# x loaded by column block and turned by VectorE, with single shares and half low pieces, in a fused GRU and mixture FFN kernel

## The chip, the cores and the metric

The kernel runs on one core of a Trainium2 chip. The metric is device time in microseconds of one execution; the median of three runs of the kernel before is 142.57 us (142.33 to 142.85). The engines that the text speaks of are TensorE (PE, with PEld for its weight loads), VectorE (DVE), ScalarE (ACT), GpSimd (POOL) and SyncE (SP), which here only issues DMAs.

## The reference

The input x has 32 sequences of 32 steps and 256 features. A GRU runs over the steps, and a feed-forward layer with routing is applied to the hidden states; x is added to its result.

```python
def cell(h, x):
    gi = x @ W_ih + b_ih
    gh = h @ W_hh + b_hh
    ...
    r = jax.nn.sigmoid(i_r + h_r)
    z = jax.nn.sigmoid(i_z + h_z)
    n = jnp.tanh(i_n + r * h_n)
    h_new = (1.0 - z) * n + z * h
...
probs = jax.nn.softmax(xt @ w_router, axis=-1)
topk_p, topk_idx = jax.lax.top_k(probs, TOPK)
...
gate = (xt @ w_gate).reshape(T, K, I)
up = (xt @ w_up).reshape(T, K, I)
basis = jax.nn.silu(gate) * up
...
out = out + shared
...
x = x + _L0_ffn_ref(_L0_cond_ref(cond_2048, x, ...), ...)
```

Here the batch is 32, the hidden size 256, there are 128 experts over 8 basis blocks of 128, and the best 4 are taken.

## The kernel before

The GRU is a chain of 32 steps. The state lies with 32 rows for each of four column blocks of 64 (j = 0 to 3), so that all 128 partitions are used. In a step t, `h_part` on TensorE (L618) adds h @ W_hh to a PSUM bank `gates` that already holds the part of x and the biases; ScalarE takes the tanh of two gates (`trz`, L415); VectorE makes `m` (L867), `pre` (L870) and the blend (`sc_add`, L873); ScalarE takes a second tanh (L422); VectorE runs a scan that blends (L879), transposes the new state into `hT` (L886) and halves it (`hhalf`, L887). Then the next `h_part` can start.

The feed-forward layer works on chunks of four steps, 128 rows. It trails the GRU by six steps: what `filler` puts on TensorE begins in step 6 with the `logits` (L651) and the first `unit` (L639). Each unit multiplies with a high and a low piece of the weights: ScalarE rounds a piece of `wraw` into `whi` (`hi_pieces`, L433), and VectorE (`lo_piece`, L899) or GpSimd (L341) subtracts it into `wlo`. The tables HI_AT, LO_VECTOR_AT and LO_POOL_AT say in which step which piece is made.

Steps 0 to 5 have no feed-forward work, and TensorE uses them to multiply x with W_ih ahead for the 18 steps in EARLY (`early_x_pair`, L597, two steps to a PSUM bank). VectorE adds the biases to each pair and keeps it in `early` (`keep_early`, L854); ScalarE loads it back into a `gates` bank in time. For the other steps `x_part` (L582) does this in the step before.

x comes in by chunks of four steps as `xtok` (L247), one row of 1 KB to a partition, eight loads of 128 KB. For the products it has to be turned: TensorE transposes a chunk with an identity (`turn_x`, L557), chunks 2 to 7 in pairs in steps 1 to 3, and VectorE (L832, L838) or, for one pair, ScalarE (L409) copies it into `xT`. `xtok` is also what the residual adds at the end (L996).

The order on each engine is written out by hand: in step t every engine does its part of the step, then `prepare(t)`, then the part of the feed-forward layer that trails. DMAs go over two hardware queues, SyncE's and ScalarE's, in program order: SyncE loads the first chunk of x, half of W_ih, W_hh in two parts, the second chunk, then waits for its half of W_ih, loads the other chunks, the router and the weights; ScalarE loads the other half of W_ih, the two biases and the first state `h0`. Before step 0, TensorE runs matmuls on zeros (`keep_warm`, L772), the x parts of steps 0 and 1 and the spreading of the biases over the banks (L550).

## Time and profile before

| | us |
|---|---|
| median of three runs | 142.57 (142.33 to 142.85) |
| the profiled execution | 142.47 |
| its span in the trace | 140.7 |
| start of step 0's h_part | 9.34 |
| start of step 6's h_part | 29.42 |

The span is what the trace covers, from the first instruction to the last; 1.8 us of the execution lie around it. The stages are read best one behind the other: loading up to 9.34 us, six steps of the GRU with the shares of x up to 29.42, then GRU and feed-forward layer together up to about 121, and the last chunk. In a table by stage each engine has its busy time and its count of instructions; PEclk is the clock that was granted, as a share of the full 2.4 GHz, and the DMA share is the mean over the core's 16 DMA engines. In a timeline a row has its start, its duration and, in brackets, how long the engine had been idle and what ended that. Durations of instructions that follow each other overlap a little, so what one costs its engine is the distance to the next start, called a slot here.

### The profile page before, as it was taken

Reading aid. Unit: us, or ns where it says so; the run is one execution under the profiler, and the core shown is the slowest. Engines: PE = TensorE matmul, PEld = TensorE weight load, DVE = VectorE, ACT = ScalarE, POOL = GpSimd, SP = SyncE. Lnnn points to the kernel's source line nnn. Section 1 sums busy time; section 2 is a strip of 40 time slices with the busy share of each in tenths; the row PEclk is TensorE's granted clock in tenths of the full one; section 3 lists DMA queues with packets and bytes.
Section 4 is the critical chain, followed back from the end, with each engine's and each line's share of the span. In section 5 each row is a group of like instructions: output and inputs, shape, how many; then the busy total and the mean of one; then the engine's idle time right before and its main releaser. Section 6 shows DMA issues by size and latency. Waiting matters only on the chain.

```text
span 140.7 us, 4037 instructions
## 1 busy us (share of the span) xinstructions
PE 135.4 (96%) x1485; PEld 98.3 (70%) x1485; DVE 105.4 (75%) x387; ACT 73.3 (52%) x246; POOL 70.0 (50%) x127
## 2 busy tenths in 40 slices
PE   6998999999999999999999999999999999999981
PEld 5455677666677667777777777777767776888880
DVE  1227699998779989885888588858885888686661
ACT  1214764667855565565556545655555554442930
POOL 5031165666656676534554454455545544885130
PEclk9999999999999999999999999999999999999997
DMA  4999980000000000000100010001000000010102
GB/s 127 315 298 306 310 301 13 0 5 2 0 5 0 0 2 5 2 0 5 37 0 0 5 37 0 9 0 37 0 5 0 31 11 0 2 37 0 42 0 75
DMA packets 5575, 7.12 MB, mean 51 GB/s; under 512 B 676, under 2 KB 4020, under 8 KB 5556
## 3 DMA queue, kind: packets, MB, share of 16 engines
q1 hardware_dynamic: 5184, 6.42, 13.8%
q10 hardware_dynamic: 308, 0.43, 1.2%
q8 instruction: 12, 0.20, 0.6%
q14 instruction: 7, 0.06, 0.1%
q0 software_dynamic: 64, 0.01, 0.0%
HBM read 5.81 MB, written 1.05 MB: 49 GB/s over the span
## 4 chain that ended last, share of the span: by engine, by line
PE 84%; DVE 10%; ACT 2%; issue 1%; DVEq 0%
PE unit L639 41%; PE gates L618 17%; PE gates L582 6%; PE down L701 5%; PE turned L772 3%; PE route L651 2%; DVE sc_out L879 2%; DVE early L854 2%; DVE wlo L899 2%; ACT sc_add L422 1%; PE route L674 1%; PE unit L597 1%; DVE hT L886 1%; DVE pre L870 1%; PE route L656 1%
## 5 line engine op out<-in xcount | busy, mean ns | idle before, releaser
L304 POOL CAST hThi<-hT 128x64 fp32r<-128x64 f32 x32 | 10.1, 316 | 50.5 <-DVE hT L886 50.5
L639 PE MATMUL unit<-whi,hThi 128*128 128x512 f32 x80 | 34.4, 430 | 0.0
L639 PE MATMUL unit<-wlo,hThi 128*128 128x512 f32 x80 | 31.6, 395 | 0.0
L639 PE MATMUL unit<-whi,hTlo 128*128 128x512 f32 x80 | 31.6, 395 | 0.0
L618 PE MATMUL gates<-whh,hT 128*32 128x192 f32 x512 | 27.4, 332 | 0.8 <-DVE hT L886 0.5
L415 ACT ACTIVATE trz<-gates 128x128 f32<-128x128 f32 x32 | 8.8, 276 | 24.6 <-PE gates L618 24.6
L618 PEld LDWEIGHTS gates<-whh,hT 128*32 128x32 f32 x512 | 13.4, 109 | 9.7 <-DVE hT L886 3.9
L639 PEld LDWEIGHTS unit<-whi,hThi 128*128 128x128 f32 x80 | 15.3, 192 | 6.6 <-issue 3.7
L879 DVE TENSOR_TENSOR_SCAN sc_out<-sc_mul,sc_add 128x128 f32<-128x128 f32 x32 | 14.0, 437 | 6.8 <-ACT sc_add L422 6.3
L639 PEld LDWEIGHTS unit<-wlo,hThi 128*128 128x128 f32 x80 | 15.0, 188 | 3.6
L928 DVE SCALAR_TENSOR_TENSOR p<-th,unit 128x256 f32<-128x256 f32 x40 | 15.9, 410 | 1.5 <-ACT th L443 1.5
L639 PEld LDWEIGHTS unit<-whi,hTlo 128*128 128x128 f32 x80 | 15.1, 189 | 2.1
L422 ACT ACTIVATE sc_add<-pre 128x64 f32<-128x64 f32 x32 | 10.3, 323 | 10.2 <-DVE pre L870 10.2
L316 POOL TENSOR_TENSOR qc<-q,coef 128x512 f32<-128x512 f32 x14 | 14.6, 1041 | 0.5 <-DVE q L940 0.5
L443 ACT ACTIVATE th<-unit 128x256 f32<-128x256 f32 x40 | 14.2, 370 | 1.0 <-PE unit L639 1.0
L867 DVE SCALAR_TENSOR_TENSOR m<-trz,gates 128x64 f32<-128x64 f32 x32 | 7.0, 217 | 8.5 <-ACT trz L415 8.2
L306 POOL TENSOR_TENSOR hTlo<-hT,hThi 128x64 fp32r<-128x64 f32 x32 | 11.6, 362 | 2.6
L582 PE MATMUL gates<-wih,xT 128*32 128x192 f32 x224 | 11.7, 327 | 0.0
L940 DVE SCALAR_TENSOR_TENSOR q<-p,unit 128x256 f32<-128x256 f32 x28 | 11.1, 415 | 0.5
L341 POOL TENSOR_TENSOR wlo<-wraw,whi 128x256 fp32r<-128x256 f32 x14 | 11.1, 816 | 0.0
L873 DVE SCALAR_TENSOR_TENSOR sc_add<-trz,hhalf 128x64 f32<-128x64 f32 x32 | 11.0, 343 | 0.0
L417 ACT ACTIVATE sc_mul<-trz 128x64 f32<-128x64 f32 x32 | 10.2, 320 | 1.0
(131 smaller groups left out, 238.5 us busy)
## 6 DMA issues: line engine op xcount, KB each, us to landing
xtok<-in_x_dram SPq DMA_DIRECT2D x8, 128.0 KB, 3.4
wraw<-in_L_ffn_w_gate_dram SPq DMA_DIRECT2D x2, 512.0 KB, 5.5
wraw<-in_L_ffn_w_up_dram SPq DMA_DIRECT2D x2, 512.0 KB, 6.5
out_dram<-ot SPq DMA_DIRECT2D x8, 128.0 KB, 2.0
whh<-in_L_cond_W_hh_dram SPq DMA_DIRECT2D x1, 512.0 KB, 6.2
wih<-in_L_cond_W_ih_dram ACTq DMA_DIRECT2D x1, 384.0 KB, 3.3
wih<-in_L_cond_W_ih_dram SPq DMA_DIRECT2D x1, 384.0 KB, 4.0
whh<-in_L_cond_W_hh_dram SPq DMA_DIRECT2D x1, 256.0 KB, 5.2
```

The source lines that it names most:

```text
L306: pool.tensor_tensor(hTlo[:, c % 3, :, :, k], hT[:, c % 2, :, k, :], hThi[:, c % 3, :, :, k].bitcast(F32), ALU.subtract).then_inc(hTlo_rea ...
L316: pool.tensor_tensor(qc[:, cols].rearrange("p (k i) -> p k i", i=I), q[:, p % 2, cols].rearrange("p (k i) -> p k i", i=I), coef[:, p % 2, ...
L341: last = pool.tensor_tensor(wlo[:, s, a, cols], wraw[:, s, a, cols], whi[:, s, a, cols].bitcast(F32), ALU.subtract)
L422: act.activation(by_block(sc_add, 0), natural(pre, slice(0, FJ)), ACT.Tanh).then_inc(n_ready, 1)
L443: act.activation(th[:, n % 2, :], unit_bank[n % NB][:, 0:UW], ACT.Tanh, scale=0.5)\
L582: pe.matmul(g[Q * j:Q * (j + 1), R:4 * FJ], x_block(t, s), wih[:, s, :].rearrange("p (g j c) -> p j g c", g=3, j=NJ)[:, j], start=False, s ...
L618: last = pe.matmul(g[Q * j:Q * (j + 1), HN:HN + 3 * FJ], st, whh[:, s, :].rearrange("p (g j c) -> p j g c", g=3, j=NJ)[:, j], start=False, ...
L639: last = pe.matmul(dst, st[:, p % 3, s, :, :].rearrange("p b t -> p (b t)"), w[:, s, :, cols], start=(s == 0 and n == 0), stop=(s == KB - ...
L873: dve.scalar_tensor_tensor(out=by_block(sc_add, 1), in0=natural(trz, slice(FJ, 2 * FJ)), scalar=1.0, in1=natural(hhalf, slice(0, FJ)), op0 ...
L879: dve.tensor_tensor_scan(sc_out[:, :, :].rearrange("p f a -> p (f a)"), sc_mul[:, :, :].rearrange("p f a -> p (f a)"), sc_add[:, :, :].rea ...
L928: dve.scalar_tensor_tensor(out=p1[:, n % 2, :], in0=th[:, n % 2, :], scalar=1.0, in1=unit_bank[n % NB][:, 0:UW], op0=ALU.add, op1=ALU.mult)\
L940: dve.scalar_tensor_tensor(out=dst, in0=p1[:, n % 2, :], scalar=0.5, in1=unit_bank[n % NB][:, UW:2 * UW], op0=ALU.mult, op1=ALU.mult).then ...
```

## The change

A second copy of x, `xj`, is loaded by column block: the 32 sequences of block j lie on partitions 32j to 32j + 31, with 64 floats for each step. It comes in five parts by steps (X_PARTS: 0 to 3, 4 to 7, 8 to 15, 16 to 23, 24 to 31), each by four DMAs, one to a block, in runs of 256 bytes. In this layout a transpose of 32 by 32 blocks on VectorE (`turn_x(n)`) gives `xT` directly. TensorE's transposes of x, `keep_x` and `keep_x_pair` on VectorE and ScalarE, and their semaphores are gone. `xtok` stays for the residual and is loaded last.

The first part of xj goes over both queues, two blocks each, ahead of everything else; part 1 follows W_hh on SyncE, parts 2 and 3 stand between W_ih's wait and the router, part 4 between the first and the second pair of weights.

The 18 early steps are now single shares, three in each of steps 0 to 5 (EARLY_SHARES), and the banks are handed out by a table (EARLY_BANK); VectorE keeps pairs 0 to 6 in steps 0 to 5 and pairs 7 and 8 in steps 11 and 12 (KEEP_EARLY). VectorE's three low pieces are made in halves (gate or up), over steps 3 to 6. Ahead of step 0, six warming matmuls stand where three and the first two transposes were, and the wait for the constants is behind the first products.

```diff
-EARLY_PAIRS = [[0], [1], [2], [3, 4], [5, 6], [7, 8]]
-TURN_PAIR = {1: 2, 2: 4, 3: 6}
-KEEP_PAIR_SCALAR = {1: 2}
-KEEP_PAIR_VECTOR = {2: 4, 3: 6}
+EARLY_SHARES = [[0, 1, 2], [3, 4, 5], [6, 7, 8], [9, 10, 11], [12, 13, 14], [15, 16, 17]]
+EARLY_BANK = [0, 1, 2, 0, 1, 2, 0, 3, 4]
+KEEP_EARLY = {0: [0], 1: [1], 2: [2, 3], 3: [4], 4: [5], 5: [6], 11: [7], 12: [8]}
+X_PARTS = [(0, 4), (4, 8), (8, 16), (16, 24), (24, 32)]
+TURN_X = {0: 2, 1: 3, 3: 4}
 HI_AT = [(0, 0), (0, 0), (0, 2), (2, 4), (4, 6), (6, 8), (8, 10)]
-LO_VECTOR_AT = [[], [], [], [2], [4], [5]]
+LO_VECTOR_AT = [[], [], [], [(2, 0)], [(2, 1), (4, 0)], [(4, 1), (5, 0)], [(5, 1)]]
...
+        def load_xj(queue, n, blocks=range(NJ)):
+            t0, t1 = X_PARTS[n]
+            for j in blocks:
+                queue.dma_start(xj[Q * j:Q * (j + 1), t0:t1, :], x[:, t0:t1, FJ * j:FJ * (j + 1)]).then_inc(ld_xj[n], 16)
...
-            return xT[:, t // TC, s, B * (t % TC):B * (t % TC + 1)]
+            return xT[:, s, B * t:B * (t + 1)]
...
-            load_x(sp, 0, 1)
+            load_xj(sp, 0, [0, 1])
             sp.dma_start(wih[:, 1, :], pairs(w_ih)[:, 1, :]).then_inc(ld_wih[1], 16)
             sp.dma_start(whh[:, :, 0:D], pairs(w_hh)[:, :, 2 * D:3 * D]).then_inc(ld_whh, 16)
             sp.dma_start(whh[:, :, D:3 * D], pairs(w_hh)[:, :, 0:2 * D]).then_inc(ld_whh, 16)
-            load_x(sp, 1, 2)
+            load_xj(sp, 1)
             sp.wait_ge(ld_wih[1], 16)
-            load_x(sp, 2, NC)
+            load_xj(sp, 2)
+            load_xj(sp, 3)
...
+                if pair == 0:
+                    load_xj(sp, 4)
...
+            load_x(sp, 0, NC)
...
+            load_xj(act, 0, [2, 3])
             act.dma_start(wih[:, 0, :], pairs(w_ih)[:, 0, :]).then_inc(ld_wih[0], 16)
...
-                if t in KEEP_PAIR_SCALAR:
-                    keep_x_pair(KEEP_PAIR_SCALAR[t])
...
+                pe.wait_ge(x_turned, 1 + [a <= t < b for a, b in X_PARTS].index(True))
...
+            def early_share(i):
+
+                n, a, t = i // 2, i % 2, EARLY[i]
+                dst = early_bank[EARLY_BANK[n]]
+                if i == 0:
                     pe.wait_ge(bias_ready, 1)
-                if n >= len(early_bank):
-                    pe.wait_ge(early_ready, n - len(early_bank) + 1)
-                for a, t in enumerate(EARLY[2 * n:2 * n + 2]):
-                    wait_x(t)
-                    for s in range(KB):
-                        for j in range(NJ):
-                            last = pe.matmul(dst[Q * j:Q * (j + 1), 4 * FJ * a + R:4 * FJ * (a + 1)], x_block(t, s),
-                                             wih[:, s, :].rearrange("p (g j c) -> p j g c", g=3, j=NJ)[:, j],
-                                             start=(s == 0), stop=(s == KB - 1), skip_group_check=True)
-                last.then_inc(early_raised, 1)
-
-            def turn_x_pair(c):
-                wait_x(TC * (c - 1))
-                turn_x(c, route, 0)
-                turn_x(c + 1, route, 1)
+                if a == 0 and EARLY_BANK[n] in EARLY_BANK[:n]:
+                    pe.wait_ge(early_ready, 1 + max(m for m in range(n) if EARLY_BANK[m] == EARLY_BANK[n]))
+                wait_x(t)
+                for s in range(KB):
+                    for j in range(NJ):
+                        last = pe.matmul(dst[Q * j:Q * (j + 1), 4 * FJ * a + R:4 * FJ * (a + 1)], x_block(t, s),
+                                         wih[:, s, :].rearrange("p (g j c) -> p j g c", g=3, j=NJ)[:, j],
+                                         start=(s == 0), stop=(s == KB - 1), skip_group_check=True)
+                if a == 1:
+                    last.then_inc(early_raised, 1)
...
-                if t < len(EARLY_PAIRS):
-                    for n in EARLY_PAIRS[t]:
-                        early_x_pair(n)
-                if t == 0:
-                    turn_x(1, unit_bank[2], 0)
-                if t in TURN_PAIR:
-                    turn_x_pair(TURN_PAIR[t])
+                if t < len(EARLY_SHARES):
+                    for i in EARLY_SHARES[t]:
+                        early_share(i)
...
-            pe.wait_ge(const_ready, 2)
-            turn_x(0, route, 0)
-            keep_warm(3)
+            keep_warm(WARM_LAST)
             x_part(0, [0])
             x_part(1, [0])
+            pe.wait_ge(const_ready, 2)
...
+            def turn_x(n):
+                t0, t1 = X_PARTS[n]
+                dve.wait_ge(ld_xj[n], 16 * NJ)
+                dve.transpose(xT[:, :, B * t0:B * t1], xj[:, t0:t1, :].rearrange("p t (c s) -> p s (t c)", s=KB))\
                     .then_inc(x_turned, 1)
 
-            def keep_x_pair(c):
-                dve.wait_ge(x_raised, c + 2)
-                dve.tensor_copy(xT[:, c:c + 2, :, :].rearrange("p c s (t b) -> p (c s) t b", t=TC),
-                                route[:, 0:4 * P].rearrange("p (a b t) -> p a t b", a=2 * KB, t=TC))\
-                    .then_inc(x_turned, 1)
-
-            keep_x(0)
+            turn_x(0)
             dve.wait_ge(ld_bias, 32)
...
+            def lo_half(i, a):
 
                 u, s = PIECES[i]
                 cols = slice(UW * u, UW * (u + 1))
                 dve.wait_ge(w_hi, i + 2)
-                dve.tensor_tensor(wlo[:, s, :, cols], wraw[:, s, :, cols], whi[:, s, :, cols].bitcast(F32),
+                dve.tensor_tensor(wlo[:, s, a, cols], wraw[:, s, a, cols], whi[:, s, a, cols].bitcast(F32),
                                   ALU.subtract).then_inc(w_lo, 1)
...
-                if t < len(EARLY_PAIRS):
-                    for n in EARLY_PAIRS[t]:
-                        keep_early(n)
-                if t == 0:
-                    keep_x(1)
-                if t in KEEP_PAIR_VECTOR:
-                    keep_x_pair(KEEP_PAIR_VECTOR[t])
+                if t in TURN_X:
+                    turn_x(TURN_X[t])
+                for n in KEEP_EARLY.get(t, []):
+                    keep_early(n)
...
-                    for i in LO_VECTOR_AT[t]:
-                        lo_piece(i)
+                    for i, a in LO_VECTOR_AT[t]:
+                        lo_half(i, a)
...
                 mixing_table(step)
+            turn_x(1)
```

SyncE's DMA queue from its start, before (SPq rows; `xtok` and `xj` are x, `wraw` the feed-forward weights):

```order
L247 DMA xtok<-in_x_dram 128x1x256
L256 DMA wih<-in_L_cond_W_ih_dram 128x768
L257 DMA whh<-in_L_cond_W_hh_dram 128x2x256
L258 DMA whh<-in_L_cond_W_hh_dram 128x2x512
L247 DMA xtok<-in_x_dram 128x1x256 x7
L262 DMA rraw<-in_L_ffn_w_router_dram 128x256
L266 DMA wraw<-in_L_ffn_w_gate_dram 128x2x512
L266 DMA wraw<-in_L_ffn_w_up_dram 128x2x512
```

and the same place now:

```order
L250 DMA xj<-in_x_dram 32x4x64 x2
L263 DMA wih<-in_L_cond_W_ih_dram 128x768
L264 DMA whh<-in_L_cond_W_hh_dram 128x2x256
L265 DMA whh<-in_L_cond_W_hh_dram 128x2x512
L250 DMA xj<-in_x_dram 32x4x64 x4
L250 DMA xj<-in_x_dram 32x8x64 x8
L270 DMA rraw<-in_L_ffn_w_router_dram 128x256
L274 DMA wraw<-in_L_ffn_w_gate_dram 128x2x512
L274 DMA wraw<-in_L_ffn_w_up_dram 128x2x512
```

Ahead of the first weights there are 14 loads of x where there were 8, and one more stands ahead of W_hh.

VectorE from the end of step 3 to the `m` of step 4, before:

```order
L886 STREAM_TRANSPOSE hT<-sc_out 128x2x32
L887 TENSOR_SCALAR hhalf<-sc_out 128x64
L854 TENSOR_TENSOR early<-turned,bias 128x2x192
L854 TENSOR_TENSOR early<-down,bias 128x2x192
L838 COPY xT<-route 128x512
L899 TENSOR_TENSOR wlo<-wraw,whi 128x2x256
L867 SCALAR_TENSOR_TENSOR m<-trz,gates 128x64
```

and now:

```order
L861 STREAM_TRANSPOSE hT<-sc_out 128x2x32
L862 TENSOR_SCALAR hhalf<-sc_out 128x64
L814 STREAM_TRANSPOSE xT<-xj 128x2x256
L829 TENSOR_TENSOR early<-unit,bias 128x2x192
L874 TENSOR_TENSOR wlo<-wraw,whi 128x256
L842 SCALAR_TENSOR_TENSOR m<-trz,gates 128x64
```

One `early` addition has gone, the copy has become a transpose, and the low piece is half as wide.

VectorE from the end of step 6 to the `m` of step 7, where the feed-forward layer's selection of experts (`lx`, `v`, `marked`) begins, before:

```order
L887 TENSOR_SCALAR hhalf<-sc_out 128x64
L953 TENSOR_REDUCE lx<-route 128x128
L958 MAX v<-lx 128x8
L962 MATCH_REPLACE marked<-keys,lx 128x132
L867 SCALAR_TENSOR_TENSOR m<-trz,gates 128x64
```

and now:

```order
L862 TENSOR_SCALAR hhalf<-sc_out 128x64
L874 TENSOR_TENSOR wlo<-wraw,whi 128x256
L928 TENSOR_REDUCE lx<-route 128x128
L933 MAX v<-lx 128x8
L937 MATCH_REPLACE marked<-keys,lx 128x132
L842 SCALAR_TENSOR_TENSOR m<-trz,gates 128x64
```

The last half of a low piece has moved in ahead of the selection.

## Rows read from the trace of the kernel before

**Rows 1.** By stage: engines' busy us (instructions), PEclk, DMA share, GB/s

```profile
3.50:9.34 5.84, 5.78 (x71) 2.87 (x69) 1.21 (x7) 1.11 (x2) 1.14 (x1) 1.00 0.99 321
9.34:12.27 2.93, 2.59 (x52) 1.77 (x51) 2.04 (x12) 0.92 (x3) 0.00 (x0) 1.00 0.82 232
...
33.04:36.20 3.16, 3.16 (x29) 2.10 (x33) 2.59 (x11) 2.61 (x9) 2.14 (x5) 1.00 0.00 0
36.20:121.00 84.80, 84.72 (x860) 61.39 (x860) 68.99 (x266) 47.05 (x171) 45.89 (x85) 1.00 0.02 8
```

**Rows 2.** VectorE's timeline: start, duration, engine, line, operation, tiles, [idle before]

```profile
8.97 0.25 DVE L860 STREAM_TRANSPOSE hT<-h 128x64 f32<-128x64 f32 x1 [2.85 <-DMA h<-in_cond_dram]
...
10.57 0.22 DVE L867 SCALAR_TENSOR_TENSOR m<-trz,gates 128x64 f32<-128x64 f32 x1 [0.42 <-ACT trz L415]
...
15.61 0.37 DVE L920 TENSOR_SCALAR mix<-pk,prec,scale_e 128x8 f32<-128x8 f32 x1
...
18.13 0.55 DVE L854 TENSOR_TENSOR early<-unit,bias 128x384 f32<-128x384 f32 x1
18.59 0.68 DVE L838 COPY xT<-route 128x512 f32<-128x512 f32 x1
19.19 0.72 DVE L891 TENSOR_TENSOR wrouter<-rraw,wrouter 128x256 fp32r<-128x256 f32 x1
19.83 0.21 DVE L867 SCALAR_TENSOR_TENSOR m<-trz,gates 128x64 f32<-128x64 f32 x1
...
21.48 0.55 DVE L854 TENSOR_TENSOR early<-turned,bias 128x384 f32<-128x384 f32 x1
...
23.00 1.20 DVE L899 TENSOR_TENSOR wlo<-wraw,whi 128x512 fp32r<-128x512 f32 x1
24.13 0.21 DVE L867 SCALAR_TENSOR_TENSOR m<-trz,gates 128x64 f32<-128x64 f32 x1
...
27.72 0.21 DVE L867 SCALAR_TENSOR_TENSOR m<-trz,gates 128x64 f32<-128x64 f32 x1
...
50.62 0.22 DVE L867 SCALAR_TENSOR_TENSOR m<-trz,gates 128x64 f32<-128x64 f32 x1 [0.22 <-ACT trz L415]
```

**Rows 3.** TensorE's timeline in step 4: h_part, then four shares of x

```profile
22.24 0.86 PE L618 MATMUL gates<-whh,hT 128*32 128x192 f32 x16
22.92 2.78 PE L597 MATMUL unit<-wih,xT 128*32 128x192 f32 x64
```

**Rows 4.** SyncE's timeline: issues of DMAs, start, duration, line, tiles

```profile
0.74 0.67 SPq L247 DMA_DIRECT2D xtok<-in_x_dram  x1
...
2.70 0.61 SPq L258 DMA_DIRECT2D whh<-in_L_cond_W_hh_dram  x1
3.36 5.87 SPq L247 DMA_DIRECT2D xtok<-in_x_dram  x7
...
10.51 0.61 SPq L266 DMA_DIRECT2D wraw<-in_L_ffn_w_up_dram  x1
```

**Rows 5.** DMA issues: count, KB each, us from issue to landing

```profile
whh<-in_L_cond_W_hh_dram SPq DMA_DIRECT2D x1, 512.0 KB, 6.2
```

**Rows 6.** ScalarE's timeline: its first two issues of DMAs

```profile
0.75 0.40 ACTq L387 DMA_DIRECT2D wih<-in_L_cond_W_ih_dram  x1
1.18 0.77 ACTq L389 DMA_DIRECT2D bi<-in_L_cond_b_ih_dram  x1
```

**Rows 7.** ScalarE's DMA queue from 5.2 to 8.4 us: packets, MB, engines' share

```profile
q10 hardware_dynamic: 131, 0.03, 4.5%
```

**Rows 8.** SyncE's DMA queue from 9.4 to 11 us

```profile
q1 hardware_dynamic: 450, 0.41, 86.1%
```

**Rows 9.** The DMA queues' own waits: us in total, times, longest

```profile
SPq L247 <- DMA wih<-in_L_cond_W_ih_dram: 1.5, 1, 1.5
```

**Rows 10.** DMA issues from 10.9 to 11.7 us: us to landing

```profile
wraw<-in_L_ffn_w_up_dram SPq DMA_DIRECT2D x1, 512.0 KB, 5.6
```

**Rows 11.** ScalarE's timeline: the first two high pieces

```profile
17.53 1.13 ACT L433 ACTIVATE whi<-wraw 128x512 fp32r<-128x512 f32 x2
```

More of the change, by code:

```diff
@@ L98, in build @@
         mix = sb("mix", [P, K])
-        xT = sb("xT", [P, NC, KB, TC * B])
+        xj = sb("xj", [P, T, FJ])
+        xT = sb("xT", [P, KB, T * B])
         xtok = sb("xtok", [P, NC, D])
@@ L156, in build @@
         ld_x_first = sem("ld_x_first")
+        ld_xj = [sem(f"ld_xj{n}") for n in range(len(X_PARTS))]
         ld_x = [sem(f"ld_x{pair}") for pair in range(NC // 2)]
@@ L749, in filler @@
                 if p >= 0:
-                    if k == 0 and p == 0:
-                        pe.wait_ge(x_turned, 4)
                     if k == 0:
```

37 lines of the change are left out of this document (5 added, 32 removed).

## Prediction

> **What bounds the kernel now.** I read the table by stage first. Behind step 7 TensorE has no gap: from 36.2 to 121 us it is busy 84.72 of 84.80 us [rows 1]. The change touches none of that work, so whatever moves the start of this stretch moves the end by as much. It works ahead of it: on the load phase up to 9.34 us, where the 16 DMA engines are 99% busy [rows 1], and on steps 0 to 5.
>
> Second, the chain of steps. A step on VectorE begins with the product `m` (L867). The first starts at 10.57, the sixth at 27.72 [rows 2]: five steps in 17.15 us. What a step costs with little else queued is the stage 9.34 to 12.27, 2.93 us [rows 1]. In step 3 (19.83 to 24.13, 4.30 us) VectorE is never idle: behind the step's own work it runs two `early` additions, a copy of xT and a low piece, and only then the next `m` [rows 2]. TensorE is late there too, with four shares and four transposes, but it starts step 4's h_part at 22.24 [rows 3], early enough for an `m` a good half microsecond ahead of 24.13. So in steps 2 to 5 VectorE's extra work is what ends last.
>
> Third, the start. Step 0 needs three things that come within half a microsecond: h0 (its transpose starts at 8.97, after 2.85 us of waiting for the DMA) [rows 2], W_hh (issued at 2.70, landing 6.2 later, at 8.9) [rows 4, 5], and the chain through the biases.
>
> **The change part by part.**
>
> *Steps 0 to 4 on VectorE.* From `m` to the first extra instruction a step takes 19.83 to 21.48, 1.65 us. An `early` addition holds a slot of 0.46 (18.13 to 18.59), the copy of 512 columns 0.60 (18.59 to 19.19), the router's subtraction of 256 columns 0.64 (19.19 to 19.83), the low piece of 512 columns 1.13 (23.00 to 24.13) [rows 2]. New are the transposes of xj. No row shows one of 512 columns: the bounds are the copy of as many (0.60) and eight times the 64-column transpose of 0.25, 2.0 us [rows 2]. I take 0.62, by the copy, which moves as many columns through the same engine. The Trainium skill's Vector Engine (DVE) Microarchitecture Reference, section 3.8, has the transposing front-end sustain one element per cycle and lane; no run here shows it, and by it the rival of slow transposes below would fall away. Half a low piece goes by the router's subtraction, 0.62.
> - Step 0: 1.65 + 0.62 + 0.46 = 2.73, under the chain: 2.93. TensorE's three shares (four take 2.78, so 2.1) and 0.68 for h_part [rows 3] stay under it too.
> - Step 1: 1.65 + 0.62 + 0.46 + 0.37 (`mix`) [rows 2] = 3.10.
> - Step 2: 1.65 + 2 × 0.46 + 0.64 = 3.21.
> - Step 3: 1.65 + 0.62 + 0.46 + 0.62 = 3.35.
> - Step 4: 1.65 + 0.46 + 2 × 0.62 = 3.35.
>
> The five make 15.94 against 17.15: **1.2 us gained**. With the transpose at its other end, 2.0 us, steps 0, 1 and 3 turn this into a loss of 2.7. TensorE's transposes of x, ScalarE's copy in step 1 and VectorE's copies are gone, and these sums are without them.
>
> *The transpose ahead of step 0.* turn_x(1), 256 columns, goes into the 0.42 us that VectorE waits for ScalarE before the first `m` [rows 2]; by half the copy and a fixed part it needs 0.35 to 0.4. Nothing, but without cover: if xj's second part lands late, `m` and all of step 0 stand behind that wait.
>
> *Given back behind step 5.* One half piece now stands in step 6, ahead of the reduction of the logits. There TensorE and VectorE are both full: TensorE is busy 3.16 of 3.16 us in step 7 [rows 1]. Step 5 brings VectorE there 0.3 earlier (one `early` less, two halves for one whole), the half adds 0.62: 0.2 to 0.3 late. And keep_early 7 and 8 move to steps 11 and 12. At the end of step 11 VectorE idles 0.22 before the `m` at 50.62 [rows 2], so 0.46 more costs 0.25, on a step where TensorE waits for the chain; in step 12 the same 0.46 hides behind TensorE. Together **0.45 back**, with 0 and 0.8 as ends.
>
> *The start.* On ScalarE's queue two loads of xj now stand ahead of W_ih, the biases and h0; one issue there holds 0.40 to 0.77 us [rows 6], so those three are issued about 1.1 later. The table load behind them slips too and is not waited for. On SyncE's queue one more load stands ahead of W_hh: 0.6 later. If issue sets the landings, step 0 starts up to 1.1 later. If the packets set them, only the pieces count: x's first four steps come as 512 packets of 256 bytes in place of 128 of 1 KB. 131 packets, h0's, took 4.5% of 16 engines in 3.2 us, 17.6 ns each [rows 7]; 450, nearly all 1 KB of x, took 86.1% in 1.6 us, 49 ns each [rows 8]. (512 × 17.6 − 128 × 49)/16 = 0.17 us. The engines are 99% busy [rows 1], so I stay nearer to the packets: **0.4 later**, from 0.2 to 1.1.
>
> *The weights.* Ahead of `up`, the second load of the first weights, issued at 10.51 [rows 4], stood 13 issues on SyncE and a wait of 1.5 us for W_ih [rows 9]; now 19, and the wait mostly passes while issuing. At 0.62 each (seven in 5.87, less the 1.5) [rows 4, 9] it is issued at 0.74 + 19 × 0.62 = 12.5, and 5.6 later [rows 10], at 18.1, it lands. ScalarE's copies of the first pieces started at 17.53 [rows 11] and fall due at about 18.0 (0.4 for the start, 0.1 for step 1). Step 3's tanh needs ScalarE at 19.9, and the copies take 1.13, so a landing up to 18.75 costs nothing: hidden, with 0.65 of cover. The second pair, 25 issues deep, goes out at 16.2 and lands at about 21.8; step 4 asks for it at about 24.6. xtok, now last, is wanted from step 16 on.
>
> *TensorE's warming* (six matmuls in place of three and two transposes) lies in the wait for W_ih: nothing.
>
> **Sum**, against the profiled execution (142.47 us: a span of 140.7 and 1.8 around it; 0.1 under the median of 142.57): 142.47 − 1.2 + 0.45 + 0.4 = 142.1.
>
> **The rivals.**
> 1. *Everything goes through.* The small pieces cost the start nothing, and steps 6 and 11 hide their additions: 142.47 − 1.2 = 141.3, to 140.8 if steps 1 and 2 come down toward the chain. For it: x needs no TensorE, PSUM or identity any more. Against: three landings within half a microsecond.
> 2. *Issue or small pieces decide the start.* h0 and the biases land 1.1 later: 142.47 − 1.2 + 0.45 + 1.1 = 142.8. For it: the two extra issues are real. The Trainium skill, DMA: Bandwidth & Descriptors, Specifications, asks for 512 bytes or more at line rate; by it a 256-byte packet costs like one of 512, an estimate of 24.5 ns from [rows 8], and the sum would be 142.3. The measured 17.6 ns speaks for less.
> 3. *SyncE's queue makes the first weights late: slower.* Place: ScalarE's first high piece, in step 2. It decides once the issues hold more than 0.65 us each, since 19 of them then use up the cover. At 0.70 `up` lands at 19.6, 0.9 too late: 143.0. At 0.75 (single issues hold 0.67 on SyncE, 0.77 on ScalarE [rows 4, 6]) it lands at 20.6: 143.9. Against: seven loads of x at 0.62.
> 4. *Transposes go by their blocks.* At 2.0 us for 512 columns the sum is 142.47 + 2.7 + 0.85 = 146.0; at 1.3, 144.0.
>
> **How the numbers follow.** Forecast 0.42, rival 1 0.22, rival 2 0.16, rival 3 0.14, rival 4 0.06. About 0.3% (0.43 us) is what a measurement of this kernel can tell from no change: faster means under 142.14, slower over 143.0. The forecast's own ends (0.2 to 0.8 for the start, 0 to 0.8 given back) reach from 141.5 to 142.9: 0.22 faster, 0.20 within. Rival 1 is faster; rival 2 lies half within, half over; rivals 3 and 4 are slower. Faster 0.44, within 0.28, slower 0.28. Range 141.0 to 143.4: it leaves out the best end of rival 1 and the far parts of 3 and 4, under 0.2 in all.
>
> **What would show it.** Right: h_part of step 0 starts near 9.75; the `m` rows of steps 0 to 5 lie 2.9, 3.1, 3.2, 3.35 and 3.35 apart; the first logits start 0.8 earlier than before; steps 7 and 12 each give back 0.2. Wrong: ScalarE's first high piece (L440) waiting for a DMA (rival 3); transposes of 512 columns at 1 us or more (rival 4); VectorE waiting for xj between the steps, which the sum has at nothing; or TensorE losing more than 0.5 us behind step 6.

## The result, and the profile after

| | before | after |
|---|---|---|
| median, us | 142.58 (142.33 to 142.85) | 145.44 (143.38 to 146.62) |
| profiled execution, us | 142.47 | 145.53 |
| its span | 140.7 | 143.5 |

The changed kernel is slower: ratio 1.0144, 95% interval 1.0103 to 1.0185; by the two medians it is 1.020. The prediction said 142.1, and 143.4 at most. Ratios, here and below, leave out every run that is more than 1.5% above the fastest of its kernel: 146.62 here, two of four in e12, one of eight in e13 and eight of twelve in e15, while e2 and e9 have no ratio because only one run of each would be left. In the changed start TensorE's clock falls to half in some executions and not in others, and such a fall costs about 2 us, so the mean granted clock over the span is given where times are compared. The four runs of the changed kernel had 0.976 (145.53), 0.998 (146.62), 0.988 (145.36) and 0.996 (143.38). The record of the clock can read 1.00 while matmuls take half-clock times, as e12 shows below; whether that was so at 146.62 isn't known.

TensorE's timeline of the kernel after (start, duration, line, operation, idle before):

```profile
6.76 0.86 PE L574 MATMUL gates<-wih,xT 128*32 128x192 f32 x16 [1.43 <-DMA wih<-in_L_cond_W_ih_dram]
...
8.06 1.85 PE L555 MATMUL gates<-bsum,pick 4*32 4x256 f32 x16
9.83 1.51 PE L574 MATMUL gates<-wih,xT 128*32 128x192 f32 x16
...
12.24 1.51 PE L606 MATMUL gates<-whh,hT 128*32 128x192 f32 x16
...
16.22 0.82 PE L606 MATMUL gates<-whh,hT 128*32 128x192 f32 x16
...
55.54 0.86 PE L606 MATMUL gates<-whh,hT 128*32 128x192 f32 x16
```

The same engine before:

```profile
5.76 0.89 PE L582 MATMUL gates<-wih,xT 128*32 128x192 f32 x16
...
7.04 1.04 PE L550 MATMUL gates<-bsum,pick 4*32 4x256 f32 x16
...
9.34 0.86 PE L618 MATMUL gates<-whh,hT 128*32 128x192 f32 x16
...
12.27 0.86 PE L618 MATMUL gates<-whh,hT 128*32 128x192 f32 x16 [0.34 <-DVE hT L886]
...
52.76 0.86 PE L618 MATMUL gates<-whh,hT 128*32 128x192 f32 x16
```

These rows hold the whole balance. The first x part starts 1.0 later (6.76 against 5.76), for TensorE stands idle 1.43 us until W_ih lands. From there to step 0's h_part it takes 5.48 us against 3.58: 1.9 more, since the same matmuls take 1.85 and 1.51 where they took 1.04 and 0.86. Step 0 takes 3.98 against 2.93: 1.05 more. From step 1's h_part to step 13's it takes 39.32 against 40.49: 1.17 *less*. Together 2.8 us, the difference of the spans. So the steps gained about what they were to gain, and the start lost more than twice that.

By stage (us, busy us of PE, PEld, DVE, ACT, POOL, PEclk, DMA share, GB/s), after, against [rows 1]:

```profile
6.00:8.00 2.00, 1.23 (x24) 0.83 (x28) 0.49 (x3) 0.00 (x0) 0.00 (x0) 1.00 0.99 324
8.00:10.00 2.00, 2.00 (x27) 0.85 (x20) 0.00 (x0) 0.38 (x1) 1.14 (x1) 0.55 1.30 205
...
12.00:14.00 2.00, 2.00 (x26) 1.15 (x28) 0.20 (x1) 0.18 (x1) 0.00 (x0) 0.50 1.03 277
14.00:16.00 2.00, 2.00 (x44) 1.34 (x40) 1.55 (x7) 0.72 (x3) 0.18 (x1) 0.74 1.07 328
```

The granted clock is 0.50, the 1.2 GHz level, from soon after 8 us to about 15, behind the idle stretch that ends at 6.76. Before, it is 1.00 there [rows 1]; TensorE had no such stretch in the start.

VectorE's timeline after, against [rows 2]:

```profile
4.09 0.45 DVE L814 STREAM_TRANSPOSE xT<-xj 128x256 f32<-128x256 f32 x1 [2.65 <-DMA xj<-in_x_dram]
6.99 0.18 DVE L819 COPY bsum<-bh 4x64 f32<-4x64 f32 x1 [2.46 <-DMA bh<-in_L_cond_b_hh_dram]
...
10.67 0.24 DVE L835 STREAM_TRANSPOSE hT<-h 128x64 f32<-128x64 f32 x1 [3.19 <-DMA h<-in_cond_dram]
...
14.12 0.22 DVE L842 SCALAR_TENSOR_TENSOR m<-trz,gates 128x64 f32<-128x64 f32 x1 [1.93 <-ACT trz L422]
...
15.76 0.70 DVE L814 STREAM_TRANSPOSE xT<-xj 128x512 f32<-128x512 f32 x1
...
17.64 0.22 DVE L842 SCALAR_TENSOR_TENSOR m<-trz,gates 128x64 f32<-128x64 f32 x1 [0.73 <-ACT trz L422]
...
20.57 0.22 DVE L842 SCALAR_TENSOR_TENSOR m<-trz,gates 128x64 f32<-128x64 f32 x1
...
23.91 0.21 DVE L842 SCALAR_TENSOR_TENSOR m<-trz,gates 128x64 f32<-128x64 f32 x1
...
27.25 0.21 DVE L842 SCALAR_TENSOR_TENSOR m<-trz,gates 128x64 f32<-128x64 f32 x1
...
30.19 0.21 DVE L842 SCALAR_TENSOR_TENSOR m<-trz,gates 128x64 f32<-128x64 f32 x1
...
37.06 0.21 DVE L842 SCALAR_TENSOR_TENSOR m<-trz,gates 128x64 f32<-128x64 f32 x1
```

The `m` rows lie 3.52, 2.93, 3.34, 3.34 and 2.94 apart: 16.07 for five steps, where 15.94 was forecast and 17.15 stood before. A transpose of 512 columns takes 0.70.

ScalarE's issues after, against [rows 6], and what the DMA view of the first 6 us says (the engines' busy share in tenths and GB/s, in 40 slices of 0.15 us; packets; us from issue to landing):

```profile
0.76 0.90 ACTq L250 DMA_DIRECT2D xj<-in_x_dram  x2
1.68 0.45 ACTq L400 DMA_DIRECT2D wih<-in_L_cond_W_ih_dram  x1
...
3.08 0.64 ACTq L403 DMA_DIRECT2D h<-in_cond_dram  x1
```

```profile
DMA  0000000000015547449795354499999998899999
GB/s 0 0 0 0 0 0 0 0 0 0 0 32 128 132 104 162 92 91 190 128 200 68 56 126 143 184 389 369 369 389 369 430 369 348 328 451 333 316 348 369
DMA packets 1030, 1.05 MB, mean 175 GB/s; under 512 B 635, under 2 KB 776, under 8 KB 1030
...
wih<-in_L_cond_W_ih_dram ACTq DMA_DIRECT2D x1, 384.0 KB, 4.9
```

The same before:

```profile
DMA  0000000000089927956998999989999999797588
GB/s 0 0 0 0 0 0 0 0 0 0 0 61 102 164 102 164 205 205 246 430 451 348 376 367 437 364 355 430 369 430 355 321 296 231 243 241 217 193 241 231
DMA packets 795, 1.23 MB, mean 204 GB/s; under 512 B 152, under 2 KB 505, under 8 KB 795
...
wih<-in_L_cond_W_ih_dram ACTq DMA_DIRECT2D x1, 384.0 KB, 3.3
```

W_ih's first half is issued 0.93 later (1.68 against 0.75) and needs 4.9 us in place of 3.3. From 1.8 to 3.9 us the DMA engines move 56 to 200 GB/s; before, they were above 340 from 2.85 to 4.6. In these two microseconds the engines are busy to between 0.3 and 0.9, and mostly with small packets: of the first 6 us' packets 635 are under 512 bytes, 152 before. So W_ih is 2.5 us later in all: 0.93 by its issue, 1.6 by the longer way from issue to landing. With the later issue and the old way of 3.3 us it would have been there at 5.0, ahead of the 5.76 at which the first x part started before. What makes the way longer is taken up under order or small pieces.

### The profile page after: what moved, and what is told of

Read it like the earlier page. It is cut to its first block, busy times and chain, and to the rows that moved or that the text cites. A ratio compares the mean times of both kernels' runs of the same rounds, so it can differ in the third digit from the quotient of the medians.

```text
span 143.5 us, 4031 instructions
## 1 busy us (share of the span) xinstructions
PE 135.9 (95%) x1472; PEld 97.6 (68%) x1472; DVE 105.7 (74%) x391; ACT 72.5 (51%) x245; POOL 70.6 (49%) x127
## 3 DMA queue, kind: packets, MB, share of 16 engines
q1 hardware_dynamic: 9312, 7.41, 19.2%
HBM read 6.86 MB, written 1.05 MB: 55 GB/s over the span
## 4 chain that ended last, share of the span: by engine, by line
PE 67%; DVE 21%; ACT 4%; DMA 3%; issue 2%; ACTq 1%; DVEq 0%
PE unit L627 33%; PE gates L606 13%; PE gates L574 6%; PE down L689 4%; DVE sc_out L854 4%; DMA wih<-in_L_cond_W_ih_dram 3%; ACT sc_add L429 2%; DVE pre L845 2%; DVE early L829 2%; PE route L639 2%; DVE m L842 2%; DVE hT L861 1%; DVE xT L814 1%; DVE sc_add L848 1%; PE gates L555 1%
## 5 line engine op out<-in xcount | busy, mean ns | idle before, releaser
L606 PE MATMUL gates<-whh,hT 128*32 128x192 f32 x512 | 28.4, 338 | 1.7 <-DVE hT L861 1.5
L854 DVE TENSOR_TENSOR_SCAN sc_out<-sc_mul,sc_add 128x128 f32<-128x128 f32 x32 | 14.5, 455 | 7.0 <-ACT sc_add L429 6.3
L574 PE MATMUL gates<-wih,xT 128*32 128x192 f32 x224 | 12.4, 341 | 1.4 <-DMA wih<-in_L_cond_W_ih_dram 1.4
L318 POOL TENSOR_TENSOR hTlo<-hT,hThi 128x64 fp32r<-128x64 f32 x32 | 12.3, 385 | 2.6
L589 PE MATMUL unit<-wih,xT 128*32 128x192 f32 x224 | 10.9, 342 | 0.0
```

Of the source, the lines that this page charges most:

```text
L318: pool.tensor_tensor(hTlo[:, c % 3, :, :, k], hT[:, c % 2, :, k, :], hThi[:, c % 3, :, :, k].bitcast(F32), ALU.subtract).then_inc(hTlo_rea ...
L574: pe.matmul(g[Q * j:Q * (j + 1), R:4 * FJ], x_block(t, s), wih[:, s, :].rearrange("p (g j c) -> p j g c", g=3, j=NJ)[:, j], start=False, s ...
L589: last = pe.matmul(dst[Q * j:Q * (j + 1), 4 * FJ * a + R:4 * FJ * (a + 1)], x_block(t, s), wih[:, s, :].rearrange("p (g j c) -> p j g c", ...
L606: last = pe.matmul(g[Q * j:Q * (j + 1), HN:HN + 3 * FJ], st, whh[:, s, :].rearrange("p (g j c) -> p j g c", g=3, j=NJ)[:, j], start=False, ...
L854: dve.tensor_tensor_scan(sc_out[:, :, :].rearrange("p f a -> p (f a)"), sc_mul[:, :, :].rearrange("p f a -> p (f a)"), sc_add[:, :, :].rea ...
```

## The experiments

Three theories. **Order**: what counts is that W_ih, the biases and h0 are issued behind the loads of xj. **Small pieces**: 256-byte pieces slow whatever moves beside them. **Clock**: TensorE's idle stretch brings the half clock, which doubles the loss.

### Start or steps

*e4_first_by_pe*, the start alone undone:

```diff
-            load_xj(sp, 0, [0, 1])
+            load_x(sp, 0, 1)
-            load_xj(act, 0, [2, 3])
-            keep_warm(WARM_LAST)
+            turn_first()
+            keep_warm(3)
-            turn_x(0)
+            dve.tensor_copy(xT[:, :, 0:P]..., route[:, 0:2 * P]...)
```

> The start alone is undone: x's first chunk is loaded in 1 KB rows at the head of SyncE's queue and turned by TensorE, as in the kernel before, and the first part of xj is not loaded; the steps behind it are those of the changed kernel. If the whole loss is in the start and the gain in steps 0 to 5 is real, h_part of step 0 starts near 9.4, m of step 5 comes 15.5 to 16 us behind that of step 0, and the time is 142.5 - 1.2 - 0.4 to 142.5 - 1.2 + 0.45, so 140.9 to 141.8: faster than either kernel. If the loss stands elsewhere (the many small loads behind the start, SyncE's queue), it is 143.5 or more. If xj's second part lands too late for its transpose ahead of step 0's m (it landed at 11.2 in the changed kernel), step 0 waits up to 1 us: 142.0 to 142.8.

Measured: 143.12, ratio 1.0017 [0.9991, 1.0043], granted clock 1.0 in all four runs; the forecast of 140.9 to 141.8 missed. The loss is gone, but the gain does not come through: step 0's h_part starts at 10.02, for W_hh landed 7.2 us after its issue in place of 6.2, and `m` waited for xj's second part. From there to step 13 (52.85) it takes 42.83 against 43.42: 0.6 gained, 0.7 lost at the start.

*e12_start_alone*, the kernel before with the changed start and nothing else:

```diff
-            load_x(sp, 0, 1)
+            load_xj(sp, [0, 1])
+            load_xj(act, [2, 3])
-            turn_x(0, route, 0)
-            keep_warm(3)
+            keep_warm(6)
-            keep_x(0)
+            dve.transpose(xT[:, 0, :, :], xj...)
```

> The kernel before with the change's start alone: x's first four steps by four column-block loads over the two queues ahead of the weights, turned by VectorE, six matmuls of warming in place of three and two transposes; the steps, the early pairs and the low pieces as before. If the start holds the whole loss, W_ih lands near 6.6, h0 is turned near 10.6, h_part of step 0 starts at 11.0 (full clock) to 12.3 (half clock), and with the steps unchanged the time is 142.8 + 1.7 = 144.5 to 142.8 + 2.9 = 145.7, so as slow as the changed kernel or slower by the 0.6 that the steps gained there. If the loss needs the rest of the change (the 24 small loads behind the start), h_part of step 0 starts below 10.5 and the time is under 143.8.

Measured: 146.96 (145.13 to 147.62), ratio 1.0215 [1.0163, 1.0266], above the forecast of 144.5 to 145.7. The start alone loses at least as much as the whole change. That the steps bring part of it back is what one expects (1.5 us by the medians, 0.7% by the ratios), but the two intervals overlap. TensorE's timeline of it:

```profile
4.24 1.49 PE L780 MATMUL turned<-empty 128*128 128x256 bf16 x6
...
6.60 1.51 PE L590 MATMUL gates<-wih,xT 128*32 128x192 f32 x16 [0.87 <-DMA wih<-in_L_cond_W_ih_dram]
...
13.16 1.51 PE L626 MATMUL gates<-whh,hT 128*32 128x192 f32 x16
```

All matmuls from 6.60 to the h_part at 13.16 take the half-clock times, although the granted clock of this trace reads 1.00: the record can miss the half clock, and the durations then tell it. The six matmuls on zeros ahead of the gap take them already (1.49 us here, 0.82 in e2), so in this execution the half clock didn't come from the gap of 0.87.

### The clock

*e1_warm*, the changed kernel with TensorE kept busy until W_ih is there:

```diff
-WARM_LAST = 6
+WARM_LAST = 18
```

> TensorE's matmuls that only keep it busy, behind the last of the biases' wait, rise from 6 to 18, so that it does not stand idle 1.43 us for W_ih; nothing else changes. If the half clock from 8.2 to 15.0 us comes from that idle stretch (the clock theory), the granted clock stays 1.0 through the start, the products of the biases and of x take the 1.04 and 0.86 us of before in place of 1.85 and 1.51, and h_part of step 0 starts when h0 is turned, near 11.05 in place of 12.31; step 0 itself takes 2.95 in place of 3.52. That makes 1.3 + 0.55 = about 1.8 less than the profiled run of the changed kernel, 143.7. If the queues alone hold the start (the order theory), the clock is a bystander and h_part of step 0 stays near 12, the time near 145.4.

Measured: 143.63 (143.26 to 144.38), ratio 1.0064 [1.003, 1.0098], clock 0.982 in the profiled run, 0.997 to 1.0 in the others. Twelve matmuls on zeros bring back 1.8 us by the medians, 0.8% (1.1 us) by the ratios. TensorE's timeline:

```profile
4.23 2.16 PE L754 MATMUL turned<-empty 128*128 128x256 bf16 x18
6.61 0.86 PE L574 MATMUL gates<-wih,xT 128*32 128x192 f32 x16 [0.23 <-DMA wih<-in_L_cond_W_ih_dram]
...
11.11 1.51 PE L606 MATMUL gates<-whh,hT 128*32 128x192 f32 x16 [0.65 <-DVE hT L835]
```

The chain through the biases runs at full clock and is done by 10.5, but now h0 comes last (turned at 10.80), and in this execution the clock fell behind that gap of 0.65. W_ih is as late as in the changed kernel, and step 0's h_part starts at 11.11, 1.8 later than before: by this profile 1.8 of the 2.9 that the start lost are the late loads', here h0's, and 1.1 the clock's. In step 0 the clock costs more on top (3.98 us from h_part to h_part, against 2.93 at full clock in e14).

*e2_sp_only* and *e7_sp_warm*, all four loads of x's first steps on SyncE, and the same with 21 matmuls of warming:

```diff
-            load_xj(sp, 0, [0, 1])
+            load_xj(sp, 0)
-            load_xj(act, 0, [2, 3])
```

> All four loads of x's first four steps stand on SyncE's queue; ScalarE's queue is that of before, with W_ih's first half, the biases and h0 at its head. By the order theory W_ih's first half is issued near 0.75 and lands near 4.5 in place of 6.6, h0 is turned near 9 to 9.5 in place of 10.67, and h_part of step 0 starts at 10.0 to 10.5 (W_hh, now behind four loads, may then be the last to come, near 10.5): 143.0 to 143.6. By the small-pieces theory (256-byte pieces hold up whatever is moved beside them, wherever they stand) W_ih still lands near 6.5 and h_part of step 0 starts near 12: 145.

> The kernel with all four loads of x's first four steps on SyncE's queue, and TensorE's matmuls that only keep it busy raised from 6 to 21, so that they cover the 1.84 us for which TensorE stood idle until x's first part was turned. That kernel had one run at 142.95 with a granted clock of 0.998 and three at 145.4 to 146.1 with 0.970 to 0.988. By the clock theory the idle stretch brings the half clock in most executions: now all of them lie at 142.8 to 143.3 with a clock of 0.995 or more. If the spread has another cause (the transfers themselves come late in some executions), times of 145 and more are still among them, at full clock.

Measured for e2: one run at 142.95 (clock 0.998), three at 145.42 to 146.06 (0.970 to 0.988). For e7: ten runs from 142.86 to 144.42, median 143.28, ratio 1.0041 [1.0017, 1.0065], clock 0.997 or more in all ten. The idle stretch goes, and the upper group (145.42 to 146.06) goes with it. Four of the ten lie above the forecast's 143.3 all the same, at full clock; in the profile, the slowest of them (144.42), step 0 waits 1.23 us for W_hh. TensorE's row of e2, then of e7:

```profile
6.79 0.86 PE L573 MATMUL gates<-wih,xT 128*32 128x192 f32 x16 [1.84 <-DVE xT L813]
```

```profile
6.89 0.86 PE L573 MATMUL gates<-wih,xT 128*32 128x192 f32 x16 [0.38 <-DVE xT L813]
```

The row of e2 is from the execution at 142.95: an idle stretch of 1.84 us that brought no fall. So the fall follows such a stretch often, not always, and the changed kernel's runs spread by it. What the order theory says of the loads held in e2: W_ih's first half no longer comes last, h0 is turned at 7.14, and step 0's h_part starts at 10.34. Its time did not follow, for the median is 145.58, no better than the changed kernel's. What is still a microsecond late there is x itself, whose fourth load is issued at about 2.2 and lands at 6.3.

### Order or small pieces

*e5_rows_first* and *e6_rows_all*: the same loads of xj in whole rows of 1 KB, for the first part and for all parts:

```diff
-xj[Q * j:Q * (j + 1), t0:t1, :], x[:, t0:t1, FJ * j:FJ * (j + 1)]
+xj[Q * j:Q * (j + 1), t0:t1, :]..., x[B // NJ * j:B // NJ * (j + 1), t0:t1, :]...
```

> The changed kernel, but the four loads of x's first four steps fetch as many bytes in whole rows of 1 KB (32 pieces each in place of 128 of 256 bytes); queues, issues, bytes and waits are the same. The values in xj's first part are then other values of x, so the output isn't the reference's; the work is the same. By the order theory (what counts is that W_ih and h0 are issued behind these loads) W_ih's first half still lands near 6.5, h0 is turned near 10.5, and h_part of step 0 starts no earlier than 11, later if the clock falls. By the small-pieces theory the first part of x lands a good microsecond earlier, W_ih by 5.5, TensorE hardly waits for it, h0 is turned near 9.5 and h_part of step 0 starts at 9.8 to 10.3: 142.8 to 143.3.

> As the run before it, and the later parts of xj too come in whole rows (1 KB or more a piece); again other values of x in xj, the same work and the same count of loads. If the small pieces behind W_hh on SyncE's queue slow what is in flight beside them, W_hh's second load, 6.8 us in the changed kernel, falls to about 6.2, and xj's second part lands near 9.5 in place of 11: h_part of step 0 then starts at about 9.6 to 10, and the time is 142.0 to 142.8. If the loads' count and order decide, both rows kernels give the same time.

Measured: 148.0 and 148.2, ratios 1.0376 [1.034, 1.0412] and 1.0372 [1.0348, 1.0395]. Four times larger pieces make it slower. But the edit changes two things, for these loads also take longer to issue. ScalarE's issues in e5:

```profile
0.74 2.00 ACTq L251 DMA_DIRECT2D xj<-in_x_dram  x2
2.78 0.48 ACTq L404 DMA_DIRECT2D wih<-in_L_cond_W_ih_dram  x1
```

Issuing these two loads holds the queue 2.00 us in place of 0.90, W_ih goes out at 2.78 in place of 1.68, and lands 4.5 later (4.9 in the changed kernel): 1.1 lost by the issue, 0.4 won on the way. The biases (6.99 to 8.79) and h0 (10.67 to 11.41) slip behind it, TensorE idles 2.49 us, and its matmuls from 7.41 to step 0's h_part at 14.54 take half-clock times.

Over all profiles the way of W_ih's first half from issue to landing sorts by its place: 3.2 to 3.3 us at the head of ScalarE's queue with x's first chunk in rows of 1 KB (before, e4, e8 to e11, e13, e15), 3.6 to 3.9 at the head with column blocks on the other queue (e2, e3, e7), 4.5 behind two loads in 1 KB pieces (e5, e6), 4.8 to 5.2 behind two in 256-byte pieces (the changed kernel, e1, e12, e14). So the place on the queue is the larger part, and a smaller one for the pieces, 0.3 to 0.7 us, isn't excluded. Whether the place counts because a queue's loads follow each other or for another reason, no run here shows.

*e3_act_last*, ScalarE's two loads of xj behind h0:

```diff
-            load_xj(act, 0, [2, 3])
             act.dma_start(wih[:, 0, :], ...)
...
             act.dma_start(h0[:, :], ...)
+            load_xj(act, 0, [2, 3])
```

> ScalarE's two loads of x's first four steps go behind W_ih, the biases and h0 on its queue; SyncE's two stay at the head of its own. By the order theory W_ih and h0 come as in the kernel before give or take 0.5 (h0 turned near 9.3), x's last two blocks are there by about 6, and h_part of step 0 starts near 9.8 to 10.3: 142.8 to 143.4. By the small-pieces theory nothing is gained over the changed kernel, h_part of step 0 near 12: 145. By the clock theory the time hangs on whether TensorE waits more than a microsecond for x's last blocks: if it does, the clock falls to half again and 1.5 to 2 us stay lost.

Measured: 150.74, ratio 1.0575 [1.0529, 1.0621]. The forecast of 142.8 to 143.4 missed: x's last two blocks, issued from 2.78 on, took 5.9 us in the median, and VectorE could turn x only at 10.13, not by 6. TensorE's row:

```profile
10.63 1.51 PE L574 MATMUL gates<-wih,xT 128*32 128x192 f32 x16 [5.12 <-DVE xT L814]
```

The two loads that were put last pay here, and TensorE needs all of them to begin.

### The order inside step 0

*e8_early_first*, e4 with VectorE's additions ahead of its transposes:

```diff
+                for n in KEEP_EARLY.get(t, []):
+                    keep_early(n)
                 if t in TURN_X:
                     turn_x(TURN_X[t])
-                for n in KEEP_EARLY.get(t, []):
-                    keep_early(n)
```

> The kernel with x's first chunk turned by TensorE (the start undone), and VectorE's additions of early shares go ahead of the transposes of xj in steps 0, 1 and 3. There step 0 took 3.49 us from m to m, because ScalarE's load of the gates waits for the first addition, which stood behind a transpose. If that is the cause, step 0 takes 2.93 to 3.05, h_part of step 2 comes 0.45 earlier against step 0, and if TensorE leaves it, the time falls by up to 0.4, to 142.7. If TensorE's three shares hold step 0 (they end at 12.8 there, h_part of step 1 starts at 13.0), nothing changes.

Measured: step 0 takes 2.92 from `m` to `m` (12.14 to 15.06) where e4 took 3.49. ScalarE's row of e4, then of e8:

```profile
14.22 0.39 ACT L417 ACTIVATE gates<-early 128x256 f32<-128x256 f32 x1 [2.07 <-DVE early L839]
```

```profile
14.44 0.39 ACT L417 ACTIVATE gates<-early 128x256 f32<-128x256 f32 x1 [1.47 <-DVE early L839]
```

ScalarE stood 2.07 us for the addition, with the tanh of step 1 queued behind that load of the gates. From the first `m` to the sixth it takes 15.49, where e4 took 16.06. The time did not follow: 143.0, ratio 1.0004 [0.9981, 1.0028], where 142.7 was forecast. In its profile step 0's h_part starts later, at 10.57 (h0 turned at 9.45, half clock from 8 to 11 us). No idle stretch of more than 0.28 us stands between its first matmul and that fall, so the idle stretch isn't the only way to the half clock.

### A version to beat both

*e9_two_by_pe* (e8 with x's second chunk too turned by TensorE, ahead of step 0) and *e10_start_as_before* (that chunk turned in step 0, as before, and shares moved to suit; the shares shown are e10's alone):

```diff
-            load_xj(sp, 1)
+            load_x(sp, 1, 2)
...
-EARLY_SHARES = [[0, 1, 2], [3, 4, 5], [6, 7, 8], [9, 10, 11], ...
+EARLY_SHARES = [[0, 1], [2, 3, 4], [5, 6, 7], [8, 9, 10, 11], ...
```

> The kernel of the run before it with x's second chunk too loaded in 1 KB rows and turned by TensorE, ahead of step 0, and copied by VectorE there; only the steps from the ninth on go through xj. Small pieces then come only behind the wait for W_ih. If the small pieces made W_hh late in the kernel with one chunk turned by TensorE (it landed at 9.9 there, 8.9 before), h_part of step 0 goes back to 9.4, and m of step 0 no longer waits for xj: 0.6 to 0.7 earlier than there. With the gain of the steps, less what TensorE takes back behind step 6, that is 141.5 to 142.3, faster than either kernel. If W_hh stays late, it is the order of the queue and not the small pieces: 142.5 or more.

> The start and step 0 of the kernel before (x's first two chunks in 1 KB rows, turned by TensorE, the second one in step 0, two early shares there), and from step 1 on the change: xj for the steps from the ninth on, turned by VectorE behind the additions, single shares (3, 3, 4, 3, 3), low pieces in halves. By the theory that the start alone lost the time and the steps' gain is real, h_part of step 0 starts at 9.4, m of step 5 comes 15.6 to 16.0 behind that of step 0 (17.15 before), h_part of step 7 starts 0.8 to 1.3 earlier than before, and 0.2 of it goes back in step 12: 141.8 to 142.3 where the kernel before takes 142.9, a ratio of 0.992 to 0.996. If TensorE takes back what VectorE gains (steps 6 to 9 are full on it), the ratio is 1.0.

Measured for e9: 144.8 in the median, with one run of four at 142.38; in its profile TensorE idles 1.31 us for the second chunk, issued at 3.36 behind W_hh and there at 10.7, and the clock falls; 141.5 to 142.3 was forecast. For e10, where 141.8 to 142.3 was forecast: 142.5 (141.94 to 143.4), ratio 0.998 [0.9951, 1.0009]. Step 0 starts at 9.49, and step 7's h_part at 32.54, 0.5 ahead of before. TensorE's timeline of e10 and its DMA queues from 20.3 to 21.8 us show where the rest went:

```profile
21.71 0.53 PE L613 MATMUL gates<-whh,hT 128*32 128x192 f32 x8
23.18 0.53 PE L613 MATMUL gates<-whh,hT 128*32 128x192 f32 x8 [0.93 <-issue]
```

```profile
q1 hardware_dynamic: 436, 0.54, 101.1%
q8 instruction: 1, 0.02, 4.6%
```

In the middle of step 4's h_part TensorE stops 0.93 us for nothing that the profile shows; a 16 KB load of instructions is under way while x's second load fills the engines. *e11_second_load_later* holds that load back, *e13_h0_pool* moves h0 to GpSimd's queue, *e15_both* does both, and *e14_after_h0_pool* does the second in the changed kernel with 18 matmuls of warming:

```diff
+            sp.wait_ge(hT_ready, 7)
             load_x(sp, 2, NC)
```

```diff
-            act.dma_start(h0[:, :], ...)
+            pool.dma_start(h0[:, :], ...)
```

> The kernel with the start and step 0 of before, with one wait added: the second load of x (xtok from the third chunk on, six loads of 128 KB) is issued on SyncE only once step 5 has made its state, near 28 us, in place of 18 to 23. In that kernel's trace TensorE stood for 0.93 us in the middle of step 4's h_part with no releaser that the profile shows, while a 16 KB load of instructions was under way and the 16 DMA engines were full with these loads. If the second load of x holds the instructions up (the collision theory), the stop is gone, m of step 4 comes 3.3 to 3.4 behind that of step 3 in place of 4.07, the runs of 143.1 to 143.4 disappear, and the median is 141.9 to 142.2. If the stop is chance, or comes from the weights' loads, the median stays at 142.5 and the spread from 141.9 to 143.4.

> The kernel with the start and step 0 of before and the change from step 1 on, with h0's load taken from the end of ScalarE's queue to the head of GpSimd's. GpSimd's loads landed 4 to 5 us after their issue in the profiles so far, so h0 should land by 6.5 in every execution. If h0's landing (6.9 to 11 in profiles of kernels with the same queue) makes the spread of that kernel, its runs of 143 and more disappear and the median is 141.9 to 142.2, a ratio of 0.993 to 0.996. If W_hh or the clock makes the spread, the median stays near 142.5 and runs of 143.2 to 143.4 stay among them.

> The kernel with the start and step 0 of before and the change from step 1 on, with both edits: h0's load at the head of GpSimd's queue, and x's second load issued only once step 5 has made its state. If the two late arrivals (h0, and the instructions that stood behind x's second load) are what spread that kernel's runs, h_part of step 0 starts at 9.5, m of step 4 comes 3.4 behind that of step 3, and the median is 141.9 to 142.2, a ratio of 0.993 to 0.997. If the granted clock or other transfers spread them, the median is 142.5 or more and some runs lie above 143 with a clock under 0.99.

> The changed kernel with 18 matmuls of warming and with h0's load at the head of GpSimd's queue in place of the end of ScalarE's. The kernel with 18 matmuls alone had h0 turned at 10.8, h_part of step 0 at 11.1 behind 0.65 us of idle TensorE, then half clock for step 0, and 143.6 in the median. If h0 standing behind xj and W_ih is what is left of the loss, h_part of step 0 starts at 10.1 to 10.4 (behind the chain through the biases) at full clock, and the time is 142.3 to 142.9. If W_hh is as late as h0 (it landed at 9.6 to 9.8 there), the start is no earlier than 10.5 and the time 143 or more.

Measured: e11 142.96, ratio 1.0012 [0.9991, 1.0033]; e13 142.84, ratio 1.0005 [0.9968, 1.0042]; e15 144.46 in the median (141.72 to 146.22, clock 0.968 to 0.988 in ten of twelve), ratio 0.9991 [0.9939, 1.0044] by the four runs that are left; e14 144.31, ratio 1.0118 [1.0082, 1.0154]. None of the four came down to its forecast (141.9 to 142.2, for e14 142.3 to 142.9). The stop in step 4 is in the profiles of e10 and e13 (0.93 and 0.83) and in neither profile with the load held back. But it is in none of e4, e8, e9 and e14 either, where the load isn't held back; in e8 the load of instructions and x's second load meet from 20.3 to 21.8 us as in e10, without a stop. So the collision isn't shown, and the stop stays unexplained. What came instead, in e11 and e15:

```profile
10.95 0.24 DVE L851 STREAM_TRANSPOSE hT<-h 128x64 f32<-128x64 f32 x1 [4.74 <-DMA h<-in_cond_dram]
```

```profile
7.04 0.18 DVE L835 COPY bsum<-bh 4x64 f32<-4x64 f32 x1 [1.34 <-DMA bh<-in_L_cond_b_hh_dram]
```

In e11 h0 is late; in e15, with h0 out of the way, the biases are, at 7.04 against 5.64 in e10. In e14 h0 comes early and step 0 still starts at 11.33, since the 18 matmuls take 3.22 us there (2.16 in e1) and the biases land at 7.9. So h0 alone isn't what the warm-up left over; the whole group behind xj on that queue is late. No version beats the kernel before by more than the measurement tells. Left open: why the same small loads on the same queue land anywhere in some 4 us from one execution to the next (h0 is turned at 6.88 in e10 and at 10.95 in e11, issued within 0.1 us of each other), and why the kernel before spreads so much less.

## Why the prediction was wrong

1. **Steps 0 to 4: the sum right, in part by luck.** 1.2 gained was forecast; the five `m` distances give 17.15 − 16.07 = 1.08, in e4 17.15 − 16.06 = 1.09. The transpose of 512 columns holds a slot of 0.63 in e4 (12.96 to 13.59) where 0.62 was taken from the copy; rival 4 is out. One step was off: step 0 took 3.49 in e4, not 2.93. The working counted VectorE's slots and did not see that ScalarE waits for the addition behind the transpose (e8). Steps 1 and 4 came in below their sums (2.93 for 3.10, 2.94 for 3.35) and made up for it: in step 4 a half low piece held 0.42, not 0.62.
2. **Given back: 0.3 for the 0.45 forecast.** From the sixth `m` to the eighth it takes 6.87 us (30.19 to 37.06) against 6.65 before: 0.22, where 0.2 to 0.3 was forecast. For steps 11 and 12, where 0.25 was forecast, the three distances from the twelfth `m` to the fifteenth are 9.77 against 9.68: 0.1. Part of the first goes by a way that the working did not have: a scan of VectorE that took 0.42 now takes 0.72 in steps 5 and 6, beside a subtraction of GpSimd. The rows in e4, VectorE's and GpSimd's:

```profile
28.34 0.72 DVE L864 TENSOR_TENSOR_SCAN sc_out<-sc_mul,sc_add 128x128 f32<-128x128 f32 x1
```

```profile
27.17 1.61 POOL L354 TENSOR_TENSOR wlo<-wraw,whi 128x256 fp32r<-128x256 f32 x2
```

   The scan ends 0.28 after the subtraction does. The Trainium skill (SBUF — State Buffer, section SBUF: two separate sides) has the two engines lock a shared port pair for a whole instruction when VectorE reads two inputs from SBUF; this trace agrees.
3. **The start: the step that failed.** It was put at 0.4, from 0.2 to 1.1, and measured 2.9. With the clock kept up (e1's profile) it is still 1.8, so the late loads alone are beyond the range. The working had the right issues (1.1 later on ScalarE's queue; 0.93 measured) and set them aside, because the engines were 99% busy [rows 1] and packets looked like the price. That row is a mean that starts at 3.50 us. In the two microseconds ahead of it, where the new loads stand, the engines are not full. And it had nothing for the longer way of a load that stands behind others: W_ih's took 1.6 us more, and h0 was turned 1.7 later (10.67 for 8.97) though issued 0.8 later (3.08 for 2.27), if one profile each can be trusted for a load whose landing varies as much as h0's. Nor did the term follow the late W_ih to TensorE: it priced h0's wait alone.
4. **The warming: failed.** "Lies in the wait for W_ih: nothing" was true of the time of six matmuls and missed what their end does: the wait became 1.43 us of idle TensorE and then seven at half clock. e1 puts this part at 1.8 us by the medians, 1.1 by the ratios. No rival had it.
5. **The rivals.** Rival 2 was nearest in mechanism: late issues that hold up the start, and with them 142.8. It had the later issue and not the longer way behind it; with the 1.8 of e1 for the clock it would have been 144.6. The Trainium skill (DMA: Bandwidth & Descriptors, Specifications), whose rule on pieces under 512 bytes stood beside it, is at most a smaller part here: with 1 KB pieces W_ih's way was 0.4 shorter, and it came later still by its issue. Rival 3 did not come: `up` was issued at 11.14, not 12.5, and ScalarE's first high piece doesn't wait for a DMA.
